# A decoder layer on one core: in its third attention, every fourth low half of the probabilities moves from VectorE to GpSimd, GpSimd's input splits are issued in steps, and x is loaded four batches ahead

## The reference, cut to what matters

```python
x = layernorm(x + attention_lora(x))               # causal, 16 heads of 32, weights with LoRA parts
h = layernorm1(x + mha(x, x, x))                    # self attention with biases
h = layernorm2(h + mha(h, ctx, ctx))                # cross attention over 750 context rows
h = layernorm3(h + relu(h @ fc1 + b) @ fc2 + b)
x = layernorm(x + h)
x = layernorm(x + bitlinear(gelu(bitlinear(x))))    # ternary weights, activations rounded to 8 bits
# mha: softmax(Q K^T / sqrt(32)) V per head;  x: 16 batches x 224 rows x 512;  ctx: 16 x 750 x 512
```

## Time and profile before

| what | value |
|---|---|
| median of 3 runs | 3295.54 us (3294.05 to 3306.85) |
| the profiled execution, its time and its span | 3310.13 us, 3308.3 us |
| PE busy | 3046.4 us, 92% |
| VectorE busy | 2597.7 us, 79% |
| ScalarE busy | 2037.8 us, 62% |
| GpSimd busy | 1259.3 us, 38% |
| mean granted TensorE clock | 0.972 |

### The profile page before, as it was taken

One profiled execution on the slowest core, in us unless ns is written; L12 is line 12 of the kernel. 1 busy time (PEld: TensorE's weight loads), 2 busy tenths in 40 slices (PEclk: granted clock), 3 DMA queues, 4 the chain that ended last, 5 costly groups with the idle time before them and its releaser, 6 DMA issues.

```text
span 3308.3 us, 88047 instructions
## 1 busy us (share of the span) xinstructions
PE 3046.4 (92%) x35152; PEld 2417.0 (73%) x35152; DVE 2597.7 (79%) x4750; ACT 2037.8 (62%) x4650; POOL 1259.3 (38%) x1140
## 2 busy tenths in 40 slices
PE   7998999998999868999999999999989999999996
PEld 5888888887889846878777787877756556565562
DVE  5777788888889857989999899998855766666666
ACT  2665556666778636778777777777754535444342
POOL 0454421126665743344444434343222222232222
PEclk9999999998999988999999999999989999999998
DMA  3666654445654545556565555555342121122212
GB/s 105 180 182 213 184 174 137 141 134 181 180 162 144 166 113 124 147 134 147 128 144 134 123 142 135 140 135 109 97 172 56 52 55 45 45 52 52 55 39 48
DMA packets 447334, 405.93 MB, mean 123 GB/s; under 512 B 272496, under 2 KB 354544, under 8 KB 445776
## 3 DMA queue, kind: packets, MB, share of 16 engines
q1 hardware_dynamic: 446672, 400.04, 45.2%
q10 hardware_dynamic: 256, 0.26, 0.0%
HBM read 239.98 MB, written 109.52 MB: 106 GB/s over the span
## 4 chain that ended last, share of the span: by engine, by line
PE 50%; DVE 18%; DMA 14%; ACT 8%; SPq 5%; issue 4%; POOL 1%; ACTq 0%; DVEq 0%; POOLq 0%
PE at_ps L765 21%; PE at_ps L1424 4%; PE at_ps L907 4%; PE at_ps L887 4%; PE at_ps L850 4%; DVE at_p L991 4%; DVE at_mx_cross L984 3%; PE at_ps L1438 3%; PE at_ps L1449 3%; DMA causal_spill<-at_proj 3%; PE at_ps L1405 2%; DMA self_spill<-at_proj 2%; ACT at_ps L941 2%; DVE at_proj L977 2%; DMA at_o_raw<-at_values 2%
## 5 line engine op out<-in xcount | busy, mean ns | idle before, releaser
L991 DVE TENSOR_TENSOR at_p<-at_ps,at_p 125x448 f16<-125x448 f32 (+1 forms) x1280 | 775.9, 615 | 150.3 <-ACT at_ps L941 143.9
L940 ACT ACTIVATE at_p<-at_ps 125x448 f16<-125x448 f32 (+1 forms) x1280 | 697.3, 545 | 284.5 <-PE at_ps L887 255.7
L941 ACT ACTIVATE at_ps<-at_ps 125x448 f32<-125x448 f32 (+1 forms) x1280 | 699.7, 547 | 0.0
L984 DVE TENSOR_REDUCE at_mx_cross<-at_ps 128x1 f32<-128x750 f32 x512 | 476.3, 930 | 28.0 <-PE at_ps L850 25.2
L1064 POOL TENSOR_TENSOR at_o_sum<-at_o_raw 128x256 f32<-128x256 f32 x192 | 120.9, 630 | 902.1 <-ACT at_o_raw L947 902.1
L887 PE MATMUL at_ps<-at_stacks 97*112 97x224 f16 (+2 forms) x1792 | 325.9, 258 | 22.6 <-DMA at_stacks<-at_mrow 22.0
L907 PE MATMUL at_ps<-at_values,at_p 112*128 112x33 f16 (+3 forms) x7168 | 318.1, 185 | 21.2 <-ACT at_o_raw L947 9.5
L907 PEld LDWEIGHTS at_ps<-at_values,at_p 112*128 112x128 f16 (+1 forms) x7168 | 282.9, 97 | 46.8 <-DVE at_p L991 19.4
L1472 ACT ACTIVATE at_masks<-at_ps,at_b_cols 128x256 f32<-128x256 f32 x224 | 106.7, 476 | 335.8 <-PE at_ps L1405 335.7
L987 DVE TENSOR_REDUCE at_mx<-at_ps 128x2 f32<-128x448 f32 x512 | 303.8, 609 | 9.1 <-PE at_ps L862 7.3
L1405 PE MATMUL at_ps<-at_xt,at_early 128*128 128x256 f16 x1792 | 301.9, 276 | 7.9 <-ACT at_w_first L1473 5.0
(11 more groups left out here) (196 smaller groups left out, 6702.0 us busy)
## 6 DMA issues: line engine op xcount, KB each, us to landing
at_x_res<-x SPq DMA_DIRECT2D x124, 256.0 KB, 3.1
cross_spill<-at_proj SPq DMA_DIRECT2D x64, 487.0 KB, 3.4
at_x_rows<-x SPq DMA_DIRECT2D x92, 256.0 KB, 4.5
at_prep<-bit SPq DMA_DIRECT2D x32, 512.0 KB, 4.8
at_early<-ctx SPq DMA_DIRECT2D x32, 512.0 KB, 5.3
at_stacks<-cross_spill SPq DMA_DIRECT2D x64, 243.5 KB, 3.7
causal_spill<-at_proj SPq DMA_DIRECT2D x64, 224.0 KB, 2.2
at_stacks<-causal_spill SPq DMA_DIRECT2D x128, 112.0 KB, 2.3
```

What stands on the lines that cost most here:

```text
L940: act.activation(mem.p_hi[0:self.KC, n % 4, :], scores, ACT.Exp, scale=EXP_SCALE)
L941: act.activation(scores, scores, ACT.Exp, scale=EXP_SCALE).then_inc(self.exp_done, 1)
L984: dve.tensor_reduce(self.mx[:, at, t, h:h + 1], mem.ps_qk[:, :, 0:self.KT // 2], AX.XY, ALU.max).then_inc(self.max_done, 1)
L991: dve.tensor_tensor(mem.p_lo[0:self.KC, n % 4, :], mem.ps_st[0:self.KC, self.st_bank(b, g, n), 0:2 * T], mem.p_hi[0:self.KC, n % 4, :], AL ...
```

## The change

Four things are changed; no matmul is added or taken away.

1. In the third attention the low half of pairs 3, 7 and 11 of each step is made by GpSimd. ScalarE's second exponential of these pairs goes to a new SBUF tile, `p_full`, in place of PSUM, and GpSimd reads it there. The PSUM bank is free as soon as that exponential is done. A semaphore of its own, `pool_lo_done`, releases `V n`.
2. GpSimd's three operations of a split no longer stand at one token: the first stays, the second and the third come after the next two `S` tokens. The wait for the transposing DMAs of the batch before moves from the first operation to the second.
3. The shift of the layer norm (now its own event) comes after the `S` token that follows `apply`.
4. In the causal and self attention `load` moves from group 0 to group 3 and loads for four batches later, not two; the first loads are placed in the start-up.

```diff
-    "causal": (("... M3 E0 V2 v0b load S0 V3",
+    "causal": (("... M3 E0 V2 v0b S0 V3",
...
-                 "M0 norm E1 S1 qka M1 S2 qkb V0 V1 M2 row E0 S3 M3 S0 v0a v0b V2 spill apply V3 stack"),
+                 "M0 norm load E1 S1 qka M1 S2 qkb V0 V1 M2 row E0 S3 M3 S0 v0a v0b V2 spill apply V3 stack"),
-    "self": (("M0 S1 residual load S2 E1 qka M1 S3 ...",
+    "self": (("M0 S1 residual S2 E1 qka M1 S3 ...",
...
-                 "S1 store qka E1 M0 S2 M1 V0 qkb spill ..."),
+                 "S1 store load qka E1 M0 S2 M1 V0 qkb spill ..."),
...
+        self.p_full = sb("p_full", [P, 2 * T])
...
+    def lo_by_pool(self, n):
+
+        return self.cross and n % 4 == 3
...
-            wait(pe, self.lo_done, m - ST_RING + 1)
+            wait(pe, *self.st_bank_released(b, g, n))
...
-            pe.wait_ge(self.lo_done, self.pair(b, g, n + 1))
+            pe.wait_ge(*self.lo_ready(b, g, n))
...
-            act.activation(scores, scores, ACT.Exp, scale=EXP_SCALE).then_inc(self.exp_done, 1)
+            full = mem.p_full[0:self.KC, :] if self.lo_by_pool(n) else scores
+            act.activation(full, scores, ACT.Exp, scale=EXP_SCALE).then_inc(self.exp_done, 1)
...
-        elif kind == "scores":
+        elif kind == "scores" and not self.lo_by_pool(n):
             dve.wait_ge(self.exp_done, self.pair(b, g, n + 1))
...
+        elif kind == "scores" and self.lo_by_pool(n):
+            pool.wait_ge(self.exp_done, self.pair(b, g, n + 1))
+            pool.tensor_tensor(mem.p_lo[0:self.KC, n % 4, :], mem.p_full[0:self.KC, :], mem.p_hi[0:self.KC, n % 4, :],
+                               ALU.subtract).then_inc(self.pool_lo_done, 1)
...
+            if not self.cross:
+                self.gpsimd(pool, "shift", b, g, n)
+        elif kind == "shift":
+            wait(pool, self.stored, 32 * b)
             pool.wait_ge(self.yg_done, b - self.NB + 1)
...
-                    at = resolve(b + (3 if layer.cross else 2))
+                    at = resolve(b + (3 if layer.cross else 4))
...
+                if kind in ("splitx", "splitc"):
+                    later += [(at[0], what[0], at[1], 0, what[1] + part) for part in (1, 2)]
+                elif token == "apply" and at[0].cross:
+                    later.append((at[0], "shift", at[1], 0, 0))
+                elif kind == "S" and later:
+                    yield later.pop(0)
+            yield from later
```

More of the change, by code:

```diff
@@ L568, in st_bank, with lo_ready, st_bank_left, st_bank_released @@
         return self.pair(b, g, n) % ST_RING
+    def lo_by_pool(self, n):
+        return self.cross and n % 4 == 3
+    def lo_ready(self, b, g, n):
+        pair = self.pair(b, g, n)
+        turn, at = divmod(pair - self.pair0, 4)
+        if self.lo_by_pool(n):
+            return self.pool_lo_done, turn + 1
+        return self.lo_done, self.pair0 + 3 * turn + at + 1 if self.cross else pair + 1
+    def st_bank_left(self, n):
+        pair = self.pair(self.b_end - 1, G - 1, n)
+        return (self.exp_done, pair + 1) if self.lo_by_pool(n) else self.lo_ready(self.b_end - 1, G - 1, n)
+    def st_bank_released(self, b, g, n):
+        pair = self.pair(b, g, n) - ST_RING
+        if pair < self.pair0 or not self.cross:
+            return self.lo_done, pair + 1
+        b_, n_ = divmod(pair - self.pair0, G * self.PAIRS)
+        g_, n_ = divmod(n_, self.PAIRS)
+        return (self.exp_done, pair + 1) if self.lo_by_pool(n_) else self.lo_ready(self.b0 + b_, g_, n_)
     def by_scalar(self, kind):
@@ L874, in tensor @@
                     pe.wait_ge(self.slots_set, 2 * g + 2)
-            m = self.pair(b, g, n)
-            wait(pe, self.lo_done, m - ST_RING + 1)
+            wait(pe, *self.st_bank_released(b, g, n))
             bank = self.st_bank(b, g, n)
@@ L1045, in gpsimd @@
-            pool.wait_ge(self.x_hi_done, 2 * at + 2)
-            pool.tensor_tensor(mem.x_parts[:, :, 1, :], rows, mem.x_parts[:, :, 0, :], ALU.subtract
-                               ).then_inc(self.x_split, 1)
+            if n == 0:
+                pool.wait_ge(self.x_rows_in[b % 2], 32 * (b // 2 + 1))
+                pool.tensor_scalar(rows, rows, S_X, 1.0, ALU.mult, ALU.mult).then_inc(self.x_hi_done, 1)
+            elif n == 1:
+                if at >= 1:
+                    pool.wait_ge(self.xt_in[(b - 1) % 2], 32 * ((at - 1) // 2 + 1))
+                pool.wait_ge(self.x_hi_done, 2 * at + 1)
+                pool.tensor_scalar(mem.x_parts[:, :, 0, :], rows, 1.0, 1.0, ALU.mult, ALU.mult).then_inc(self.x_hi_done, 1)
+            else:
+                pool.wait_ge(self.x_hi_done, 2 * at + 2)
+                pool.tensor_tensor(mem.x_parts[:, :, 1, :], rows, mem.x_parts[:, :, 0, :], ALU.subtract
+                                   ).then_inc(self.x_split, 1)
@@ L1048, in gpsimd @@
         elif kind == "split c":
-            chunks = slice(2 * n, 2 * n + 2)
-            pool.wait_ge(self.c_rows_in[n], (16 if n < 2 else 32) * (at + 1))
-            if at >= 1:
-                pool.wait_ge(self.ct_in[(b - 1) % 2], 96 * ((at - 1) // 2 + 1))
+            two, n = divmod(n, 3)
+            chunks = slice(2 * two, 2 * two + 2)
             rows = mem.c_rows[:, chunks, :]
-            pool.tensor_scalar(rows, rows, S_X, 1.0, ALU.mult, ALU.mult).then_inc(self.c_hi_done, 1)
-            pool.wait_ge(self.c_hi_done, 6 * at + 2 * n + 1)
@@ L1430, in tensor @@
             if index == 0:
-                pe.wait_ge(self.cross.lo_done, self.cross.pair_end)
+                for n in (2, 3):
+                    pe.wait_ge(*self.cross.st_bank_left(self.cross.PAIRS - 4 + n))
             wait(pe, self.g_free, index - 1)
@@ L1715, in step @@
                 yield causal, "store", b - 2, 0, 0
+            later = []
             for token in table.order[g]:
@@ L1769, in start @@
             yield from causal.unit(0)
+            yield from loads(2)
             yield from causal.unit(1)
@@ L1775, in start @@
             yield from spread(work, maxima)
+            yield from loads(3)
             for g in range(causal.ROW_AHEAD):
@@ L1809, in change @@
             yield cross, "v bias in", b0, 0, 0
-            yield cross, "split x", b0 + 1, 0, 0
-            for n in range(3):
-                yield cross, "split c", b0 + 1, 0, n
+            for part in range(3):
+                yield cross, "split x", b0 + 1, 0, part
+            for part in range(9):
+                yield cross, "split c", b0 + 1, 0, part
             yield cross, "load", b0 + 2, 0, 0
@@ L1846, in turnover @@
             yield cross, "apply", last, 0, 0
+            yield cross, "shift", last, 0, 0
             yield cross, "store", last, 0, 0
```

35 lines of the change are left out of this document (20 added, 15 removed), and 6 rows, old and new, of the table ORDERS.

## The result

| | before | changed |
|---|---|---|
| time, median (range) | 3295.61 us (3294.05 to 3306.85, 4 runs) | 3326.03 us (3324.41 to 3333.03, 4 runs) |
| ratio, 95% interval | | 1.0072 (1.0052 to 1.0092) |
| profiled execution, its span | 3310.13, 3308.3 us | 3324.41, 3322.6 us |
| VectorE and GpSimd busy | 2597.7 and 1259.3 us | 2522.7 and 1456.0 us |

The changed kernel is slower: by the ratio of runs taken side by side 0.7%, by the two medians 30 us or 0.9%. The work has moved as intended: GpSimd makes 192 low halves, and VectorE is 75 us less busy.

What follows compares the result with a forecast made beforehand. It took PE as the bound in the third attention, VectorE close behind, and DMA waits in the two attentions before. 49 - 10 - 16 = +23 us on the median of 3295.5 gave 3319 us, range 3288 to 3346.

Steps and rivals of the forecast that it cites:

- Cost of a low half: Third attention: 1.0 us on GpSimd (bounds 0.93 and 1.10) against VectorE's 0.62; VectorE relieved of 7.4 us a batch.
- Pair 7 of group 1: Third attention: its low half on GpSimd waits behind gain and shift, so V 7 is 2.65 us late in every batch.
- the walk: GpSimd's new queue followed through one third-attention batch: busy to 1730.8, gain from 1730.9, pair 7's low half done at 1736.8.
- The clock: Behind the gap at V 7 TensorE's clock falls, costing 1.7 us a batch.
- the rival without a clock price: The gap at V 7 costs no clock: 3294 us, no change; chance 0.13.
- Given back: Waits behind V 7 that go: 0.9 us a batch at M 5, 0.2 for all other maxima.
- The sum of a batch: Third attention: 2.65 + 1.7 - 0.9 - 0.2 = +3.25 us a batch.
- +49 for the third attention: 15 batches of 3.25 us each make +49 us; bounds +17 and +70.
- x: -26: x loaded early: -10 us in the causal attention and -16 us in the self attention.
- The first term: Causal attention: the nine waits for the rows of x, 10.7 us, go; counted -10 us, bounds -6 and -11.
- The second term: Self attention: spill no longer behind x's load, shorter stack waits, clock near 1.00; -16 us, bounds -2 and -35.
- GpSimd keeps up: Third attention: gain and shift do not stand in pair 7's way; faster, 3230 us; chance 0.13.

Runs made afterwards that it cites:

- no_x: The changed kernel with the early load of x put back where it was before; 3346.54 us, ratio 1.0117 to the kernel before.
- late_gain: The changed kernel with the third attention's gain moved behind S 7 and its shift behind S 8; 3284.42 us, ratio 0.9940 to the kernel before.
- x_only: The kernel before with only the early load of x added; 3284.98 us, ratio 0.9931 to the kernel before.
- late_whole_look: late_gain with the three operations of each split at one token again, run once more for its trace; one run, 3295.21 us.
- late_split: late_gain with the last step of c0's split put behind the gain and the shift behind that; 3285.43 us, ratio 0.9961 to the kernel before.

## Why the prediction was right, point by point

- **Cost of a low half.** Forecast 1.0 us, measured 1.035 (all 192 between 1.025 and 1.044). The ratio to VectorE's 0.618 is 1.67. The 1.96 of the Trainium skill (GPSIMD Engine Reference, section 3.1) would have made 1.21; these operands do not show it, and the measured ratio stands. The relief of VectorE was forecast at 7.4 us a batch; its busy time fell by 75 us, 4.7 a batch, part of which is that the normalizing takes 0.77 longer.
- **Pair 7 of group 1.** Right in mechanism, place and count. Gain started at 1730.45 (forecast 1730.9), the low half ended at 1736.29 (1736.8), and `V 7` was 2.26 us late (2.65). But the gain was not held by GpSimd's queue, as in the walk: that was free at 1727.50 + 2.13 = 1729.63, and the 0.82 us to 1730.45 are VectorE's normalizing, which took 0.77 us longer beside the split. PE lost 0.7 us by the same cause ahead of `V 7`, so that there the two nearly cancel. That the start fits so well is luck in part.
- **The clock.** Forecast 1.7 us behind every gap. Measured 1.7 behind ten of fifteen, nothing behind five, and no_x, whose 15 gaps at `V 7` are the same, has it behind ten as well. So the rival without a clock price is right in a third of the batches. Nor is 1.7 what it costs. From the start of `V 6` to the transposing of the maxima PE takes 13.71 us before; after, 15.50 in the batch without the clock's fall and 16.20 in the one with it. Before, the stretch starts at 1733.86; in the batch with the fall at 1733.71, a row shown with the result. The other ends, first before, then after without the fall and with it:

```profile
1747.57 0.38 PE L821 MATMUL at_ps<-at_ident,at_mx_cross 128*4 128x128 f32 x2
```

```profile
1657.12 0.39 PE L935 MATMUL at_ps<-at_prep,at_p 125*128 125x65 f16 x8
1672.62 0.38 PE L850 MATMUL at_ps<-at_ident,at_mx_cross 128*4 128x128 f32 x2
```

```profile
1749.91 0.38 PE L850 MATMUL at_ps<-at_ident,at_mx_cross 128*4 128x128 f32 x2
```

  Over the ten batches the clock adds 0.4 to 1.2 us to that stretch, 0.85 in the mean: waits for maxima fall into the slow time.
- **Given back.** Forecast 0.9 at `M 5` and 0.2 elsewhere. `M 5` gave its 0.88 in every batch. Before, `M 7` waited 0.59 too; that went as well where the clock fell. Where it did not, 0.67 us came back at `M 6`, and `M 7` kept 0.17:

```profile
1739.65 0.49 PE L850 MATMUL at_ps<-at_stacks 96*128 96x375 f16 x2 [0.59 <-DVE at_mx_cross L984]
```

```profile
1663.17 0.49 PE L879 MATMUL at_ps<-at_stacks 96*128 96x375 f16 x2 [0.67 <-DVE at_mx_cross L1013]
```

- **The sum of a batch.** Forecast 3.25, measured 3.25, and here luck must be called luck. At `V 7`, where the forecast has all of it, a batch loses 1.79 us five times and 2.22 to 2.98 ten times, 2.35 in the mean. Another 0.7 are lost at the maxima behind the normalizing, a place at which the prediction has nothing ("All other places have room, this one has not"). The remaining 0.2 were not traced. A gap 0.4 us too long and a clock priced too high on one side, a price left out on the other, cancel. late_gain checks it: the stretch of 13.71 us is 13.71 again in 14 of its 15 batches, and the batch is still 1.0 us above before's.
- **+49 for the third attention.** The trace has +37 against the kernel before and +44 against x_only. The smaller figure comes of two batches of before (77.85 us and 77.32) that waited for DMA and waited no more: 3.5 us each that I had left in both kernels. The sum against the kernel before was 12 us too large.
- **x: -26.** Measured -0.69%, -23 us, of which the trace has 18.5 us up to the third attention. The first term, the nine waits for the rows of x, held as waits: TensorE has none left. How much time that gave by itself isn't shown: the last transposes of the first attention's output come 8.5 us earlier in the changed kernel (694.4 against 702.9) and 2.6 in x_only. The second term named a wrong thing as cured. I expected the stack waits near 1 us and a clock near 1.00. They are 17.8 us in thirteen, the longest 2.6, where the earlier trace rows had 21.1 in nine, and the stage's clock is 0.96. The row of 780 to 1010 us, after:

```profile
PE at_ps L891 <- DMA at_stacks<-self_spill: 17.8, 13, 2.6
```

- **The sum.** 3319 forecast, 3326 measured. As the third attention had 37 in the trace and not 49, with x nearly as forecast, the sum of parts is +14 in the traces and +16 by no_x and x_only. The whole kernel's own ratio, +24 us, is above both and near the forecast's 23; the runs scatter by more than these differences, so the closeness of the last figure says little.
- **GpSimd keeps up.** As a rival it needed the gain out of pair 7's way, and late_gain made that so. It gave 3284, not 3230. The step that failed is its price, and with it the first paragraph's reading of the earlier trace rows: 2.6 us a batch of waits for VectorE were taken for what relief of VectorE could bring. Relief by a quarter of its low halves brought about 0.6 of it in late_whole_look's trace, and in every order tried another wait took that back.

## What to carry to other kernels

Before moving work onto an engine that is 40% busy, walk its queue at the one place where something short and urgent would stand behind something long and not urgent; that place, not the share, decides, and moving the long work behind the urgent is worth as much as the whole change cost. Ask as well what the longer queue will run beside: here a GpSimd instruction lying across VectorE's normalizing cost 0.7 us a batch, in a kernel that was to relieve VectorE. A row that says TensorE waits for VectorE isn't yet a sign that VectorE has too much to do: look at what VectorE itself was waiting for just before. Here it sat idle there, and taking a quarter of its low halves away left most of the waits. And when a forecast comes true to the digit, add it up by places: the batch of this one was right by errors that cancel. Here the early load of x is worth keeping (-0.7%), and the low halves are best left where they were.

## What the runs showed of the hardware

- VectorE's normalizing (a scalar operation, float32 from SBUF to SBUF, 128x512) takes 0.54 us alone and 1.26 to 1.33 us with a GpSimd instruction beside it, with one input or two; GpSimd's 1.04 us became 1.31 to 1.32 where it was second. In late_split, with nothing beside it, all 28 were at 0.54.
- Behind a gap of 2.25 us in a TensorE that is otherwise 95% busy the clock fell in ten of fifteen batches, in the changed kernel and in no_x alike: 0.72 over the 6 us from 1 us before the matmuls resume, 1.7 us of a full clock. In the other five it stayed at 1.00 behind a gap of the same length, at the same place of the order. Which batches have it no run explains. before's gaps of 1.79 and 1.89 us, for DMA, were both followed by 0.72. late_split's thirteen gaps at `V 11`, of 1.09 to 1.35 us, cost no clock: it is 1.00 from 1340 to 2260 us.
- What such a fall costs is less than 1.7 us where TensorE would have waited anyway: here 0.4 to 1.2 us a batch.
